# State-space block: order of TensorE's work, homes of z and place of the norm weights; second expert tile by token halves

## The reference

```python
zxbcdt = u @ W_in.T ; z, xBC, dt = split(zxbcdt)            # 1024, 1280, 16
x, B, C = split(silu(causal_conv1d(xBC, conv_w, conv_b)))   # 4 taps
dt = softplus(dt + dt_bias) ; A_cs = cumsum(dt * A)         # inside a chunk
Y = (C B^T * exp(A_cs[l] - A_cs[s]), s <= l) @ (x * dt)     # inside a chunk
Y += C @ state(chunk before) * exp(A_cs) ; Y += x * D
yg = Y * silu(z)
x = x + (yg * rsqrt(mean(yg*yg) + 1e-5) * norm_weight) @ W_out.T
```

## Time and profile before

| what | before |
|---|---|
| median of 3 runs (lowest, highest) | 1056.17 us (1056.07, 1056.78) |
| the profiled execution's own time | 1059.17 us |
| its span | 1057.1 us |
| busy: PE, DVE, ACT, POOL | 1039.6, 777.4, 601.4, 190.0 us |
| granted clock of PE, mean | 0.995 |
| chain that ended last | PE 93%, DVE 4%, ACT 1%, issue 1% |

### The profile page before, as it was taken

How to read it: one execution, slowest core, us unless ns; L and a number is a source line. 1 busy time by engine, 2 the same in 40 slices (tenths; PEclk the granted TensorE clock), 3 DMA queues, 4 the chain that set the end, 5 groups by cost and what they waited for, 6 DMA issues and landing times.

```text
span 1057.1 us, 15522 instructions
## 1 busy us (share of the span) xinstructions
PE 1039.6 (98%) x5773; PEld 888.1 (84%) x5773; DVE 777.4 (74%) x1659; ACT 601.4 (57%) x1089; POOL 190.0 (18%) x208
## 2 busy tenths in 40 slices
PE   7999999999999999999999999999999999999998
PEld 5888888887888888888888888888776788888887
DVE  5856777649777877777877777787567778777775
ACT  4444343334765566666556666659356466666664
POOL 4644434320000000000000000003132012222221
PEclk9999999999999999999999999999999899999999
DMA  6758676498004130043100440004450285555550
GB/s 233 244 190 289 213 240 193 134 318 289 12 1 163 59 119 1 2 169 105 65 1 8 163 159 17 1 1 181 175 214 1 90 338 181 185 195 188 186 173 21
DMA packets 64156, 145.76 MB, mean 138 GB/s; under 512 B 3889, under 2 KB 42705, under 8 KB 62673
## 3 DMA queue, kind: packets, MB, share of 16 engines
q1 hardware_dynamic: 64080, 144.77, 39.5%
HBM read 108.55 MB, written 36.21 MB: 137 GB/s over the span
## 4 chain that ended last, share of the span: by engine, by line
PE 93%; DVE 4%; ACT 1%; issue 1%; DMA 0%; POOL 0%; DVEq 0%; ACTq 0%
PE bank L546 18%; PE bank L483 16%; PE bank L589 12%; PE bank L566 11%; PE bank L464 10%; PE bank L837 9%; PE bank L591 6%; PE bank L839 4%; PE bank L646 2%; PE bank L493 1%; DVE conv_acc L1115 1%; PE bank L659 1%; PE bank L776 1%; PE bank L727 1%; DVE e_hl L1226 0%
## 5 line engine op out<-in xcount | busy, mean ns | idle before, releaser
L1044 DVE TENSOR_TENSOR pT<-bank,pT 128x512 fp32r<-128x512 f32 x272 | 184.6, 688 | 103.4 <-ACT pT L1453 101.4
L1453 ACT CAST pT<-bank 128x512 fp32r<-128x512 f32 x272 | 156.0, 593 | 142.8 <-PE bank L566 139.6
L589 PE MATMUL bank<-pT,vN 128*128 128x512 f32 (+1 forms) x544 | 225.7, 422 | 0.0
L546 PE MATMUL bank<-kT,qT_hi 128*128 128x512 f32 (+2 forms) x576 | 215.4, 393 | 2.1 <-DVE scores L988 2.1
L988 DVE TENSOR_SCALAR_CACHE_REDUCE scores<-bank 128x512 f32<-128x512 f32 x256 | 173.0, 685 | 2.0 <-PE bank L546 0.2
L566 PE MATMUL bank<-ident,scores 128*128 128x128 f32 x1072 | 161.3, 272 | 0.4 <-DVE pT L1044 0.3
L1424 ACT ACTIVATE scores<-scores,neg_max 128x1024 f32<-128x1024 f32 (+2 forms) x128 | 154.0, 1203 | 6.3 <-DVE neg_max L1000 6.3
L591 PE MATMUL bank<-pT,vN 128*128 128x256 f32 (+1 forms) x544 | 152.5, 280 | 0.0
L483 PE MATMUL bank<-w_ctx_hi,ctx_hl 128*128 128x512 f32 x512 | 145.5, 396 | 6.6 <-ACT ctx_hl L1333 6.6
L837 PE MATMUL bank<-fT_parts,e_hl 128*128 128x512 f32 x400 | 144.6, 398 | 0.1
L566 PEld LDWEIGHTS bank<-ident,scores 128*128 128x128 f32 x1072 | 127.2, 140 | 12.1 <-DVE pT L1044 1.2
(11 more groups left out here) (223 smaller groups left out, 1561.9 us busy)
## 6 DMA issues: line engine op xcount, KB each, us to landing
e_raw<-in_experts SPq DMA_DIRECT2D x51, 768.0 KB, 4.4
k_spill<-k_stage SPq DMA_DIRECT2D x16, 1024.0 KB, 4.5
v_spill<-v_stage SPq DMA_DIRECT2D x16, 1024.0 KB, 8.3
vN<-v_spill SPq DMA_DIRECT2D x16, 1024.0 KB, 5.2
kT<-k_spill SPq DMA_DIRECT2D x15, 1024.0 KB, 5.3
ctx_raw<-in_ctx SPq DMA_DIRECT2D x15, 512.0 KB, 4.1
w_raw<-in_w_qkv SPq DMA_DIRECT2D x6, 1024.0 KB, 5.0
wo_sb<-in_wo SPq DMA_DIRECT2D x4, 1024.0 KB, 9.3
```

The source lines that it names most:

```text
L546: done = e.matmul(bank[b][:, 0:n], qT[a][:, h, qt * P:(qt + 1) * P], kT[:, w, lo:lo + n], start=m == 0, stop=m == 2)
L589: e.matmul(halves[:, :, q0:L], vN[:, 0, kt, :], ring[:, :, i * L + q0:(i + 1) * L], start=kt == 0, stop=False)
L1044: e.tensor_tensor(ring[:, 1, :], bank[tb][:, :], ring[:, 0, :], ALU.subtract).then_inc(p_lo, 1)
L1453: e.copy(ring[:, 0, :], bank[tb][:, :]).then_inc(p_hi, 1)
```

## The change

- PE's order in the state-space block is new. `project_z(1, 0)` and `project_z(1, 1)` move behind the decays of the first and of the second chunk; `x_rows(0, 0)` moves ahead of the running sum; `x_rows(1, 0)` comes earlier and `x_rows(1, 1)` later. z of tt = 1 goes to banks 0 and 4, the state's first half to bank 1 instead of 0, and the bank waits follow.
- ACT only copies z of tt = 1 out (`take_z`) between the decays, and takes the silu of all 1024 channels in one instruction after the squares of the first chunk. DVE waits for that (`gated_z` 5).
- DVE's order follows PE's. The copy of the running sum stands after all taps instead of before the last two.
- POOL no longer multiplies `w_out`. DVE multiplies by `nw` where it copied the turned rows (`turn_y`), and now for all four quarters; the copy on ACT is gone.
- The second expert tile is done by halves too, with its gate part and its up part of tt = 0 on both sides of the turn of the last tokens. `main_of_e(3)` and `rest_of_e(3)` come earlier, the remainder of tile 2 is split around a LayerNorm, and the turn of the routing weights moves from behind `up(1)` to the middle of `up(2)`.

The diff, cut:

```diff
+BANK_Z = {(0, 0): 3, (0, 1): 4, (1, 0): 0, (1, 1): 4}
...
-        b = (3, 4)[c]
+        b = BANK_Z[tt, c]
-        if tt:
-            pe.wait_ge(gated_z, c + 1)
-        else:
-            pe.wait_ge(p_lo, NH * NPAIR)
+        pe.wait_ge(*((p_lo, NH * NPAIR) if tt == 0 else (bnat_st, 1) if c == 0 else (dsub_d, 2)))
...
-    project_z(1, 0)
-    pe.wait_ge(dtc, 18)
-    e.matmul(bank[5][:, 0:TT * MH], upto[:, :], dA_.rearrange("p t h -> p (t h)"), start=True, stop=True)
-    e.matmul(bank[5][:, 64:64 + MH], ones[:, :], dtb[8][:, 0, :], start=True, stop=True).then_inc(dt_mm, 1)
-    for tt in range(TT):
-        b, span = 6 + tt, slice(tt * P, (tt + 1) * P)
-        pe.wait_ge(uT_done, tt + 1)
-        pe.wait_ge(xc_done, 2)
-        e.matmul(bank[b][:, 0:P], xc[:, 8, span], xc[:, 9, span], start=True, stop=True).then_inc(gm_bt, 1)
-    pe.wait_ge(xpad_done, 4)
-    e.transpose(bank[0][:, 0:P], xc[:, 8, 0:P], ident[:, :]).then_inc(gm_bt, 1)
...
-    x_rows(0, 0, xpad_done, 3)
-    decay_rows(0, 0, 0, xpad_done, 5)
-    project_z(1, 1)
-    x_rows(0, 1, cs_done, 3)
-    decay_rows(0, 0, 1, gated_z, 3)
-    decay_rows(0, 1, 0, gated_z, 4)
-    decay_rows(0, 1, 1, gq, 1)
-    x_rows(1, 0, gq, 2)
-    for c in range(2):
-        b = (0, 2)[c]
-        pe.wait_ge(bnat_st, 1)
-        pe.wait_ge(xds_state, c + 1)
-        pe.wait_ge(xr, 2)
-        e.matmul(bank[b][:, :], b_nat[:, :], xds[:, c * 512:(c + 1) * 512], start=True, stop=True).then_inc(st_yo, 1)
-    decay_rows(1, 0, 0, xr, 4)
-    decay_rows(1, 0, 1, dsub_d, 1)
-    y_rows(0, 0, dsub_a, 1)
-    x_rows(1, 1, dsub_d, 2)
-    y_rows(0, 1, dsub_a, 2)
-    decay_rows(1, 1, 0, xr, 6)
-    decay_rows(1, 1, 1, bnat_st, 2)
...
+    x_rows(0, 0, xpad_done, 3)
+    pe.wait_ge(dtc, 18)
+    e.matmul(bank[5][:, 0:TT * MH], upto[:, :], dA_.rearrange("p t h -> p (t h)"), start=True, stop=True)
+    e.matmul(bank[5][:, 64:64 + MH], ones[:, :], dtb[8][:, 0, :], start=True, stop=True).then_inc(dt_mm, 1)
+    for tt in range(TT):
+        b, span = 6 + tt, slice(tt * P, (tt + 1) * P)
+        pe.wait_ge(uT_done, tt + 1)
+        pe.wait_ge(xc_done, 2)
+        e.matmul(bank[b][:, 0:P], xc[:, 8, span], xc[:, 9, span], start=True, stop=True).then_inc(gm_bt, 1)
+    pe.wait_ge(xpad_done, 4)
+    e.transpose(bank[0][:, 0:P], xc[:, 8, 0:P], ident[:, :]).then_inc(gm_bt, 1)
+    decay_rows(0, 0, 0, xpad_done, 5)
+    x_rows(0, 1, cs_done, 3)
+    x_rows(1, 0, gq, 2)
+    decay_rows(0, 0, 1, gated_z, 1)
+    decay_rows(0, 1, 0, gated_z, 2)
+    decay_rows(0, 1, 1, gq, 1)
+    project_z(1, 0)
+    for c in range(2):
+        b = (1, 2)[c]
+        pe.wait_ge(bnat_st, 1)
+        pe.wait_ge(xds_state, c + 1)
+        pe.wait_ge(dsub_d, 1)
+        pe.wait_ge(xr, 2)
+        e.matmul(bank[b][:, :], b_nat[:, :], xds[:, c * 512:(c + 1) * 512], start=True, stop=True).then_inc(st_yo, 1)
+    decay_rows(1, 0, 0, xr, 4)
+    y_rows(0, 0, dsub_a, 1)
+    decay_rows(1, 0, 1, bnat_st, 2)
+    decay_rows(1, 1, 0, xr, 6)
+    decay_rows(1, 1, 1, gated_z, 3)
+    project_z(1, 1)
+    y_rows(0, 1, dsub_a, 2)
...
+    x_rows(1, 1, gated_z, 4)
...
-    pe.wait_ge(pads_w_out, 9)
+    pe.wait_ge(w_out_in, 16)
...
-    def up_half(tt):
-        w, span = e_hl[0], slice(tt * P, (tt + 1) * P)
-        pe.wait_ge(e_lo, 1)
+    def up_half(j, tt, kinds=(0, 1)):
+        w, span = e_hl[j], slice(tt * P, (tt + 1) * P)
+        pe.wait_ge(e_lo, j + 1)
-            for m, b in enumerate(GATE_UP[0]):
+            for m in kinds:
+                b = GATE_UP[j][m]
...
-    up_half(0)
+    up_half(0, 0)
+    up_half(1, 0, (0,))
...
-    up_half(1)
+    pe.wait_ge(x2, 3)
+    up_half(1, 0, (1,))
+    up_half(0, 1)
...
+            if j == 2 and m == 1:
+                turn_weights_of_experts()
...
-    for j in range(NFT):
-        if j:
-            up(j)
-        else:
-            route_logits(1)
-        if j == 1:
-            pe.wait_ge(topk, 18)
-            pe.wait_ge(x2, 3)
-            for tt in range(TT):
-                done = e.transpose(bank[5][0:NE, tt * P:(tt + 1) * P], cw[:, tt, :], ident[:, :])
-            done.then_inc(rl_ct, 1)
-        if j >= DOWN_LAG:
-            down(j - DOWN_LAG)
+    def turn_weights_of_experts():
+        pe.wait_ge(topk, 18)
+        pe.wait_ge(x2, 3)
+        for tt in range(TT):
+            done = e.transpose(bank[5][0:NE, tt * P:(tt + 1) * P], cw[:, tt, :], ident[:, :])
+        done.then_inc(rl_ct, 1)
+    route_logits(1)
+    up_half(1, 1)
+    for j in range(DOWN_LAG, NFT):
+        up(j)
+        down(j - DOWN_LAG)
...
-    def layernorm(n, tt, write_to):
+    def layernorm(n, tt, write_to, between=None):
...
+        if between:
+            between()
...
-        dve.wait_ge(pads_w_out, 1)
+        dve.wait_ge(pads, 1)
...
-            if n == len(PAIRS) - 1 and j == 1:
-                dve.wait_ge(dt_mm, 2)
-                e.tensor_copy(cs[:, :, :].rearrange("p t h -> p (t h)"), bank[5][:, 0:TT * MH]).then_inc(cs_done, 1)
-                e.tensor_scalar(ncs[:, :, :].rearrange("p t h -> p (t h)"), bank[5][:, 0:TT * MH], -1.0, None, ALU.mult).then_inc(cs_done, 1)
-                dve.wait_ge(cs_done, 1)
-                e.tensor_tensor(dec0[:, :], bank[5][:, 64:64 + MH], cs[:, 0, :], ALU.subtract).then_inc(cs_done, 1)
+    dve.wait_ge(dt_mm, 2)
+    e.tensor_copy(cs[:, :, :].rearrange("p t h -> p (t h)"), bank[5][:, 0:TT * MH]).then_inc(cs_done, 1)
+    e.tensor_scalar(ncs[:, :, :].rearrange("p t h -> p (t h)"), bank[5][:, 0:TT * MH], -1.0, None, ALU.mult).then_inc(cs_done, 1)
+    dve.wait_ge(cs_done, 1)
+    e.tensor_tensor(dec0[:, :], bank[5][:, 64:64 + MH], cs[:, 0, :], ALU.subtract).then_inc(cs_done, 1)
...
-        dve.wait_ge(gated_z, 2 * tt + 2)
+        dve.wait_ge(gated_z, (2, 5)[tt])
-        e.tensor_copy(yT[:, 4 * c:4 * c + 4, tt * P:(tt + 1) * P], bank[b][:, :].rearrange("p (k t) -> p k t", k=4)).then_inc(yT_done, 1)
+        e.tensor_tensor(yT[:, 4 * c:4 * c + 4, tt * P:(tt + 1) * P], bank[b][:, :].rearrange("p (k t) -> p k t", k=4),
+                        nw[:, 4 * c:4 * c + 4].unsqueeze(2).to_broadcast([P, 4, P]), ALU.mult).then_inc(yT_done, 1)
...
+    decay_rows(0, 0)
-    decay_rows(0, 0)
+    x_rows(1, 0)
-    x_rows(1, 0)
+    y_rows(0, 0)
-    y_rows(0, 0)
-    x_rows(1, 1)
+    decay_rows(1, 1)
+    mask_rows(1, 0)
-    decay_rows(1, 1)
...
+    x_rows(1, 1)
-    mask_rows(1, 0)
+    turn_y(1, 1)
+    def rest_of_third(m0, m1):
+        src, dst = e_raw[2 % NRAW], e_hl[2 % NHL]
+        dve.wait_ge(e_hi, 3)
+        done = e.tensor_tensor(dst[:, 1, m0:m1], src[:, m0:m1, :], dst[:, 0, m0:m1], ALU.subtract)
+        if m1 == 3:
+            done.then_inc(e_lo, 1)
...
-    layernorm(5, 1, fn)
+    layernorm(5, 1, fn, between=lambda: rest_of_third(0, 1))
+    rest_of_third(1, 3)
-    rest_of_e(2)
+    rest_of_e(3)
...
-        if 1 <= j and j + 2 < NFT:
+        if 2 <= j and j + 2 < NFT:
...
-    def gate_z(tt, c):
+    def take_z(tt, c):
-        e.activation(gate[:, tt, c * 512:(c + 1) * 512], bank[(3, 4)[c]][:, :], ACT.Silu).then_inc(gated_z, 1)
-    gate_z(0, 0)
-    gate_z(0, 1)
+        e.activation(gate[:, tt, c * 512:(c + 1) * 512], bank[BANK_Z[tt, c]][:, :], ACT.Copy if tt else ACT.Silu).then_inc(gated_z, 1)
+    take_z(0, 0)
+    take_z(0, 1)
...
-    gate_z(1, 0)
-    gate_z(1, 1)
...
+    take_z(1, 0)
-        e.copy(state[:, c * 512:(c + 1) * 512], bank[(0, 2)[c]][:, :]).then_inc(bnat_st, 1)
+        e.copy(state[:, c * 512:(c + 1) * 512], bank[(1, 2)[c]][:, :]).then_inc(bnat_st, 1)
+    take_z(1, 1)
+    act.wait_ge(gated_z, 4)
+    e.activation(gate[:, 1, :], gate[:, 1, :], ACT.Silu).then_inc(gated_z, 1)
...
-    act.wait_ge(y_turned, 4)
-    act.wait_ge(yT_done, 3)
-    e.copy(yT[:, 4:8, P:2 * P], bank[2][:, :].rearrange("p (k t) -> p k t", k=4)).then_inc(yT_done, 1)
+    main_of_e(3)
...
-        if j + 3 < NFT:
+        if j and j + 3 < NFT:
...
-    e.memset(x_pad[:, :, 0:PAD], 0.0).then_inc(pads_w_out, 1)
-    pool.wait_ge(w_out_in, 16)
-    pool.wait_ge(small_in, 112)
-    for k in range(DI // P):
-        e.tensor_tensor(w_out[:, k, :], w_out[:, k, :], nw[:, k:k + 1].to_broadcast([P, DM]), ALU.mult).then_inc(pads_w_out, 1)
+    e.memset(x_pad[:, :, 0:PAD], 0.0).then_inc(pads, 1)
...
+        pool.wait_ge(xr, 6 + 2 * c)
```

More of the change, by code:

```diff
@@ L391, in build_program @@
         wx_hi_done, wx_lo_done, uT_hi, uT_lo, tap = (sem(n) for n in ("wx_hi", "wx_lo", "uT_hi", "uT_lo", "tap"))
-        uT_done, ea_done, pads_w_out, zp, gated_z = (sem(n) for n in ("uT_done", "ea_done", "pads_w_out", "zp", "gated_z"))
+        uT_done, ea_done, pads, zp, gated_z = (sem(n) for n in ("uT_done", "ea_done", "pads", "zp", "gated_z"))
         dt_mm, dtc, dt_exp, xp, xpad_done, conv, xc_done = (sem(n) for n in ("dt_mm", "dtc", "dt_exp", "xp", "xpad_done", "conv", "xc_done"))
```

## The result

| what | before | after |
|---|---|---|
| median (lowest, highest), 5 runs each | 1056.52 us (1056.07, 1056.78) | 1060.55 us (1060.4, 1061.54) |
| the profiled execution's own time | 1059.17 us | 1060.5 us |
| its span | 1057.1 us | 1058.4 us |
| busy: PE, DVE, ACT, POOL | 1039.6, 777.4, 601.4, 190.0 us | 1038.7, 776.0, 602.8, 181.2 us |

The ratio is 1.0033, with a 95% interval of 1.0022 to 1.0044, so slower by 2.3 to 4.7 us; the medians lie 4.0 us apart. The forecast was +2.4 us, 1058.6, in the range 1054.5 to 1061.5.

The account below looks back on a forecast made before the run. PE, busy 98% of the span, was taken as the bound. +1.75 (order), +1.06 (norm weights) and -3.0 (experts) made -0.2; plus 2.6 for the clock, +2.4 us on the median: 1058.6 us, range 1054.5 to 1061.5.

Parts of the forecast that it names:

- Norm weights: Convolution and turned rows: first taps 1.65 us earlier without POOL; fourth turned quarter on DVE puts 1.06 us on the path.
- New order: State-space block: PE idles 2.95 us before cs, 1.4 before project_y(0,0), which starts 1.75 us later at full clock.
- The clock: PE's clock falls to half after the gap before cs, for 3.2 or 6.6 us; priced at 2.6 us.
- Case 1: One clock fall, in the gap before cs: 1058.6 us, itself from 1056.5 to 1060; chance 43%.
- case 2: A second clock fall, after the 1.4 us wait before project_y(0,0): 2.3 us more, 1060.9 us; chance 22%.
- Experts: First logits to up(3), second tile by halves: waits and the clock fall near 837 go, -3.0 us, bounds -4.4 and +0.5.
- Loads of later tiles: Expert loop: later tiles' loads queue on SP behind the later spread of routing weights; 0 us, up to 1.
- The sum: Whole kernel: the parts come to -0.2 us at full clock, plus 2.6 for the clock, +2.4 us.
- case 4: DVE and ACT's chain starts 4.9 us sooner, cs by 791, clock holds: -2.2 us or more, say 1053.5; chance 15%.
- case 5: New 1.06 us before fn and fT idles PE twice, clock falls as before: +5.7 us, 1061.9; chance 6%.

Follow-up runs that it names:

- norm weights with order: Kernel before plus the moved norm weights and the new state-space order, experts' tiles as before: 1061.79 us, ratio 1.0047.
- cs early: Changed kernel with the copy of the running sum cs back ahead of the last two taps: 1061.71 us, ratio 1.0045.
- load first: Changed kernel with the ninth expert tile's load issued ahead of the spread of the routing weights: 1060.45 us, ratio 1.0031.
- x_rows early: Changed kernel with x_rows(1, 1) in bank 3, ahead of the last z and, on DVE, of the second y: 1059.49 us, ratio 1.0022.
- its copy: The kernel before, no edit, profiled once more: span 1055.3 us.
- z in the gap: Changed kernel with project_z(1, 0) put into the gap before cs (bank 3), copied out by ScalarE ahead of the exps: 1057.86 us, ratio 1.0007.
- the last two kernels: Changed kernel with z before cs, x_rows(1, 1) and ninth load early, fourth turned quarter on ScalarE: 1054.18 us; old order, banks and z with the rest: 1053.91 us.

## Why the prediction was right, and where it was off

- **Norm weights.** Right. The first taps took 0.88 us for two (0.87 forecast), cs came 1.55 us earlier with that alone (1.65 taken). The product costs what the copy did: yT at 825.74 took 0.69 us, and second_sum(0) stood behind it:

```profile
825.74 0.69 DVE L1174 TENSOR_TENSOR yT<-bank,nw 128x512 f32<-128x512 f32 x1 [1.40 <-PE bank L721]
826.35 0.74 DVE L1185 SCALAR_TENSOR_TENSOR x_sb<-bank,yrs,x_sb 128x512 f32<-128x512 f32 x1
```

  The stage to the logits grew by 1.12 us (1.06), and with that quarter on ScalarE in four pieces it is back at 18.77.
- **New order.** Right in mechanism and nearly in size: a gap of 2.75 (2.95) before cs, decays(0,0) on DVE 17.24 us after x_pad (forecast 17.26: 794.0 less 776.74), a wait of 1.51 (1.4, where its own figures, 813.7 less 812.4, give 1.3) before project_y. Without the clock's share I had +1.75; with the 1.3 that I gave a fall of 3.2 us that is 3.05, measured 3.43. The forecast, though, had 2.6 for the clock, so 4.35 for this stage, 0.9 too much. The cause was put one step off: I let cs alone make the gap, and the run with cs copied earlier shows that the end of the convolution makes it.
- **The clock.** Case 1 came: one fall, in the gap. It lasted 3.4 us in the profiles of after and of norm weights with order, and 6.8 in the three others with such a gap (cs early, load first, x_rows early), close to the two lengths forecast. By stages that stand beside one another the long one costs 1.17 us more than the short one (39.92 and 38.75), where I had reckoned 1.6: the long one began 1.0 us before PE's wait was over, and half of the 3.4 us more (1.7), less half of that 1.0, is 1.2. I had leaned to the long one because transposes stood behind the gap; after's clock came back with nothing but transposes running. The second wait of 1.4 us, case 2, brought no fall in any profile. By what the Trainium skill (TensorE: Matmul & The Clock Gate, Why this matters for your kernels) calls a long gap, case 2 was not to come, and there it agrees; but neither was a gap of 2.75 us to be one, and a fall followed it in each of the four profiles that have it.
- **Experts.** -3.08 us against the profiled before (forecast -3.0), and that this fits is luck: without the fall's 3.3 I had +0.3, and that came as -1.68, while the fall was worth 1.40, two errors of nearly 2 us that cancel. The profile held a fall that most runs do not have, and taking it away is worth 1.4, because a wait of 1.43 for the remainder of the fourth tile stood hidden behind it. Against an ordinary run of before the part gives 1.68. **This is the step that made the forecast too small:** I added a difference made against one profiled execution to a median 3.0 us below it, said that one fall might be the reason, and left it to the range. With 1.4 less of gain the sum would have been +3.8.
- **Loads of later tiles.** Sized at 0, at most 1; it was 1.2. I had 3.7 us of slack between DVE's work on that tile and PE's need of it. That reading was wrong: in before DVE makes the tile's remainder from 867.13 to 868.88 and PE takes it at 870.27, 1.4 us later. In the changed kernel the tile came at 865.5, and while ScalarE waits 2.6 us for it, its copies and silus of the tile before are late too, so POOL's and DVE's products, which stand ahead of the remainder of the new tile on DVE: 869.33 in place of 867.13. PE was ready at 870.7 and got it at 871.14, and its next two steps from tile to tile took 4.9 and 4.5 us instead of 4.2.
- **The sum.** +2.65 us by stages against +2.4 forecast is in part luck too: 0.9 too much for the first stage and 1.2 too little for the loop all but cancel. The medians' 4.0 carries the error of the experts' part on top.
- **The other rivals.** Faster by one mechanism (case 4) was to decide at cs before 791 in before's time; it came at 792.1 in that time, 0.75 earlier than before as forecast, and the gap stayed. A fall behind the new small waits before fn and fT (case 5) did not come.

## What to carry to other kernels

Work that waits for nobody is worth most in front of the place where TensorE will have to wait: `project_z(1, 0)` was such a filler, and moving it away from the gap cost the gap and a fall of the clock behind it. The length of a stage without a fall repeated within 0.1 us between two landmarks of the timeline, and within 0.3 in the long loop, where the whole time scatters by 2, so effects are to be forecast and proved by stages, and the profiled execution is to be compared with the others of its kernel before a difference is added to the median. And when a step comes later, every transfer that is issued behind it in the same queue comes later with it; here a load that had been ready for issue waited behind 4 MB.

## What the runs showed of the hardware that was not expected

- The clock's fall can be a matter of chance for one and the same kernel: 19 of 70 runs of before had a mean clock of 0.997 or less, at 1056.9 us of span against 1054.6. In the attention block, which all kernels share, PE waits 2.1 us near 241 us in every profile, and a fall of 3.4 us followed in 7 of 12 (before, its copy, changed, cs early, z in the gap, and the last two kernels), in the other 5 none. The five kernels whose PE waits 2.0 to 2.8 us for cs (changed, norm weights and order, cs early, load first, x_rows early) show the fall near it in each profile, and none of their 5, 4, 4, 6 and 10 runs had a mean clock above 0.998. With the gaps of 0.83 and 0.46 us that z leaves there was no fall in the profile, and no run of ten below 0.998. The mean alone can't place a fall (0.998 was the attention block's in one profile and the gap's in another), so that it came in each single run is likely, not shown.
- A fall can cost less than its length says. At 837 PE was at half clock for 6.8 us, and the stage was only 1.4 us longer, since PE would have waited 1.43 us for DVE later on. And what lies under a wait is free: the same short fall began 0.5 us before PE's wait for cs was over with norm weights and order (38.45 us for the stage), and 0.1 us after it in the changed kernel (38.75).
- The clock came back while PE did nothing but fp32 transposes: in the changed kernel they ran from 790.97 to 795.30, and the granted clock was 1.00 again at 794.5.
- DVE operations with both inputs in SBUF run slower beside POOL: the first taps 1.25 us each beside it and 0.44 without; the mask of 128x1024 took 1.98 us in the changed kernel (814.56) and 3.53 for two in before (813.46) while POOL worked on xD, and 1.22 with POOL idle. The products out of PSUM beside it did not (0.68 for xdt at 793.22, beside POOL's xds). The Trainium skill (SBUF — State Buffer, SBUF: two separate sides) gives the reason, a pair of ports that DVE and POOL take from one another for a whole instruction, and the traces agree with it as to which operations were slowed and which not.
